# Reordered borders around the feed-forward stage of a transformer block kernel

## The reference

```
x1 = ln(x) * (1 + scale1) + shift1
x  = x + gate1 * (attention(x1 @ qkv_w + qkv_b) @ out_w + out_b)      # 16 heads of 128
x2 = ln(x) * (1 + scale2) + shift2
x  = x + gate2 * (gelu(x2 @ ffn_w1 + b1) @ ffn_w2 + b2)               # 256 -> 1024 -> 256
```

## Time and profile before

| | us |
|---|---|
| median of 3 runs (lowest, highest) | 1209.67 (1206.79, 1210.87) |
| the profiled execution's own time | 1212.73 |
| its span | 1211.0 |
| PE, DVE, ACT, POOL busy | 1148.2, 740.0, 649.9, 514.8 |
| first up product to last up product of ffn1 | 536.6 to 637.2 |

### The profile page before, as it was taken

How to read it: one execution, slowest core, us unless ns; L and a number is a source line. 1 busy time by engine, 2 the same in 40 slices (tenths; PEclk the granted TensorE clock), 3 DMA queues, 4 the chain that set the end, 5 groups by cost and what they waited for, 6 DMA issues and landing times.

```text
span 1211.0 us, 22481 instructions
## 1 busy us (share of the span) xinstructions
PE 1148.2 (95%) x7600; PEld 1017.2 (84%) x7632; DVE 740.0 (61%) x1633; ACT 649.9 (54%) x1839; POOL 514.8 (43%) x590
## 2 busy tenths in 40 slices
PE   6999999999999999989997999999999999987994
PEld 5888999999999999978886788888887888776894
DVE  3566654335443454357665786777777777776667
ACT  3455444444444444454553677665766666684452
POOL 4111131113111211142335676665676688663673
PEclk9999999999999999999998999999999999999997
DMA  9200000000000002022002007930000100032637
GB/s 333 75 1 1 19 1 19 1 1 1 1 18 1 1 1 87 1 105 105 19 18 71 1 1 203 292 99 1 10 23 6 49 18 19 14 83 90 180 114 232
DMA packets 47267, 70.08 MB, mean 58 GB/s; under 512 B 4279, under 2 KB 39355, under 8 KB 46171
## 3 DMA queue, kind: packets, MB, share of 16 engines
q1 hardware_dynamic: 43747, 60.21, 16.5%
q0 software_dynamic: 3408, 8.43, 1.9%
HBM read 40.24 MB, written 29.30 MB: 57 GB/s over the span
## 4 chain that ended last, share of the span: by engine, by line
PE 77%; DVE 4%; POOL 3%; issue 2%; ACT 2%; DMA 2%; SPq 0%; DVEq 0%; POOLq 0%; ACTq 0%
PE bank L1834 12%; PE bank L2023 10%; PE bank L1871 9%; PE bank L2080 7%; PE bank L1902 6%; PE bank L2170 5%; PE bank L1862 4%; PE bank L2106 4%; PE bank L1844 4%; PE bank L2213 3%; PE bank L2137 2%; PE bank L2145 2%; PE bank L2244 2%; PE bank L1852 2%; PE bank L1964 2%
## 5 line engine op out<-in xcount | busy, mean ns | idle before, releaser
L577 POOL TENSOR_TENSOR p<-p,rinv 128x512 f32<-128x512 f32 x64 | 66.6, 1040 | 410.1 <-DVE rinv L1384 410.1
L906 ACT ACTIVATE p<-bank,nb,rq 128x128 f32<-128x128 f32 x256 | 113.9, 455 | 89.4 <-DVE nb L1605 89.4
L778 ACT ACTIVATE p<-bank,nmax 128x128 f32<-128x128 f32 x256 | 90.7, 367 | 117.2 <-DVE nmax L1372 117.2
L650 POOL TENSOR_TENSOR qr<-qr,rb 128x512 f32<-128x512 f32 x64 | 81.7, 1276 | 82.0 <-DVE rb L1559 80.8
L1834 PE MATMUL bank<-cur_hi,wqk_hi 128*128 128x512 f32 x256 | 108.8, 425 | 4.5 <-DVE cur_lo L1325 4.5
L1380 DVE COPY pt<-bank 128x512 f32<-128x512 f32 x64 | 44.2, 691 | 107.2 <-PE bank L1852 104.4
L1834 PE MATMUL bank<-cur_hi,wqk_lo 128*128 128x512 f32 x256 | 101.9, 398 | 0.0
L1834 PE MATMUL bank<-cur_lo,wqk_hi 128*128 128x512 f32 x256 | 101.8, 398 | 0.0
L787 ACT ACTIVATE o_hi<-bank,bqkv 128x512 fp32r<-128x512 f32 x64 | 44.2, 691 | 101.2 <-PE bank L1862 100.9
L1388 DVE SCALAR_TENSOR_TENSOR o_lo<-bank,bqkv,o_hi 128x512 fp32r<-128x512 f32 x64 | 48.0, 751 | 53.7 <-ACT o_hi L787 53.7
L1862 PEld LDWEIGHTS bank<-pt,v 128*128 128x128 f32 x512 | 67.2, 193 | 13.0 <-DVE pt L1380 8.5
(11 more groups left out here) (279 smaller groups left out, 3733.7 us busy)
## 6 DMA issues: line engine op xcount, KB each, us to landing
token_scratch<-empty SPq DMA_DIRECT2D x1, 17415.0 KB, 65.2
xs<-token_scratch SPq DMA_DIRECT2D x39, 129.0 KB, 2.3
wqk_raw<-in_wqk SPq DMA_DIRECT2D x8, 512.0 KB, 10.4
gate<-gates_scratch SPq DMA_DIRECT2D x8, 512.0 KB, 3.8
got_t<-expert_scratch SPq DMA_DIRECT2D x16, 256.0 KB, 5.3
w_raw<-in_w SPq DMA_DIRECT2D x2, 1408.0 KB, 5.8
xres<-in_x SPq DMA_DIRECT2D x4, 512.0 KB, 9.7
wv_raw<-in_wv SPq DMA_DIRECT2D x8, 256.0 KB, 10.5
```

Source lines behind the costliest of these rows:

```text
L577: nc.gpsimd.tensor_tensor(p1[:, h % 2], p1[:, h % 2], rinv[:, h % 2].unsqueeze(2).broadcast_to([P, GB, T]), ALU.mult).then_inc(a_pn, 1)
L650: nc.gpsimd.tensor_tensor(qr[:, s.u % 2], qr[:, s.u % 2], rb[:], ALU.add).then_inc(g_qr, 1)
L778: last = nc.scalar.activation(p1[:, h % 2, b], bank[3][:, b * T:(b + 1) * T], ACT.Exp, bias=nmax[:, h % 2, b:b + 1], accum_out=rsum[:, h % ...
L906: last = nc.scalar.activation(p2[:, (s.u - 3) % 2, j], bank[3][:, j * T:(j + 1) * T], ACT.Exp, scale=rq[:, (s.u - 3) % 4, j:j + 1], bias=n ...
```

## The change

Five parts. (a) The splitting of three halves of the feed-forward weights moves into heads 11 to 15 of attention1's last group; ACT, DVE and POOL take them there. (b) The gated bias of attention1's last group moves into heads 8 to 11, one sequence in each head. (c) At the first border PE's order is changed: up product 0 stands ahead of values product 62, up products 1 and 2 among the last two heads' work; the low part `h_lo` moves to other memory and so waits for transposes instead of a values product. (d) In the feed-forward the gated bias of a group is one product and one addition of 1024 elements a partition instead of four pairs of 256; `residual_scale` waits for the product alone, `residual_add` for the addition. That of the last group moves into steps 1 and 2 of attention2, its scaling from step 2 to 3, its addition from step 5 to 6. (e) At the second border step 0 starts with keys, queries and values, down product 30 stands behind them and down product 31 behind the queries and transposes of step 1; DVE's wait for the bias goes. Tiny activations (`load_table`) make ACT load the table of Gelu and of Exp at places of their own. The diff, cut to its core:

```diff
-        gb2 = sb("gb2", [P, D], at=W + 114 * KB)
+        gb2 = sb("gb2", [P, GB, D], at=WORK + 12 * KB)
-        h_lo = sb("h_lo", [P, 2, GT], F32R, at=WORK + 8 * KB)
+        h_lo = sb("h_lo", [P, 2, GT], F32R, at=WORK + 16 * KB)
...
# POOL
+            def sequence_bias(g, b):
+                pool.wait_ge(d_gate, 16 * (g + 1))
+                if b > 0:
+                    pool.wait_ge(r_b, GB * g + b)
+                nc.gpsimd.tensor_tensor(gb1[:], gate[:, b], obias[:], ALU.mult).then_inc(r_gb, 1)
+                xs = xres[:, bass.ds(g * GB + b, 1), :].rearrange("p a d -> p (a d)")
+                pool.wait_ge(r_gb, GB * g + b + 1)
+                nc.gpsimd.tensor_tensor(xs, xs, gb1[:], ALU.add).then_inc(r_b, 1)
+            def gated_bias(g):
+                pool.wait_ge(d_small, 16 * 5)
+                pool.wait_ge(d_gate, 16 * (NG + g + 1))
+                if g > 0:
+                    pool.wait_ge(r_b, BIASED + g)
+                nc.gpsimd.tensor_tensor(gb2[:], gate[:], obias[:].unsqueeze(1).broadcast_to([P, GB, D]),
+                                        ALU.mult).then_inc(r_gb, 1)
+            def add_bias(g):
+                pool.wait_ge(r_gb, BIASED + g + 1)
+                xg = xres[:, g * GB:(g + 1) * GB]
+                nc.gpsimd.tensor_tensor(xg, xg, gb2[:], ALU.add).then_inc(r_b, 1)
...
+                    if g == NG - 1 and 8 <= h < 8 + GB:
+                        sequence_bias(g, h - 8)
+                    if g == NG - 1 and h == 12:
+                        pool.wait_ge(w_hi2, 1)
+                        nc.gpsimd.tensor_tensor(w1_lo[:, 0:NF // 2], w1_raw[:, 0:NF // 2],
+                                                w1_hi[:, 0:NF // 2].bitcast(F32), ALU.subtract).then_inc(w_lo2, 1)
-            pool.wait_ge(w_hi2, 1)
-            nc.gpsimd.tensor_tensor(w1_lo[:, 0:NF // 2], w1_raw[:, 0:NF // 2], w1_hi[:, 0:NF // 2].bitcast(F32),
-                                    ALU.subtract).then_inc(w_lo2, 1)
             normalise(NG * H - 1, 1)
-            residual_bias(NG - 1, NG - 1, gb1)
...
-            for g in range(NG):
-                pool.wait_ge(d_small, 16 * 5)
-                residual_bias(NG + g, g, gb2)
-                if g < NG - 1:
-                    norm(2 * NG + g, True)
+            for g in range(NG - 1):
+                gated_bias(g)
+                add_bias(g)
+                norm(2 * NG + g, True)
...
+                if s.first and s.u == 1:
+                    gated_bias(NG - 1)
+                if s.first and s.u == 2:
+                    add_bias(NG - 1)
...
# ACT
+                    if g == NG - 1 and h in (11, 12, 14):
+                        split2((h - 11) // 2, (h - 11) % 2 if h < 14 else 0)
...
+            def load_table(kind):
+                nc.scalar.activation(table[:], eps[:], kind)
...
-            split2(0, 0)
             act.wait_ge(n_ev, 2 * (NG + 1))
             act.wait_ge(a_vp, n)
             cur(NG, 0)
             exps(n - 1, 1)
-            split2(0, 1)
+            act.wait_ge(consts, 3)
+            load_table(ACT.Gelu)
             o_hi(n - 2, H - 2)
-            split2(1, 0)
...
                     if s.first:
                         h_round(NG * NF - 1, NF - 1, False)
+                        load_table(ACT.Exp)
...
-                    if s.first and s.u == 0:
-                        act.wait_ge(f_dp, NG * NF)
+                    if s.first and s.u == 4:
+                        act.wait_ge(r_b, BIASED + NG)
...
                 if i == 7:
+                    load_table(ACT.Exp)
                     logits_copy(NG - 1, bank[6])
...
# DVE
             def residual_scale(r, j):
-                dve.wait_ge(r_b, GB * (r + 1))
+                if r < NG:
+                    dve.wait_ge(r_b, GB * (r + 1))
+                else:
+                    dve.wait_ge(r_gb, BIASED + r - NG + 1)
...
             def residual_add(r, g):
+                if r >= NG:
+                    dve.wait_ge(r_b, BIASED + r - NG + 1)
...
+                    if g == NG - 1 and h in (13, 15):
+                        split2((h - 13) // 2, (15 - h) // 2)
...
             o_lo(n - 2, H - 2)
-            split2(0, 1)
             p_t(n - 1)
-            split2(1, 0)
-            o_lo(n - 1, H - 1)
...
-                elif f == 0:
-                    dve.wait_ge(a_pvp, n - 2)
+                else:
+                    dve.wait_ge(a_tp, n - 1 + f)
...
                 if s.first and s.u == 0:
-                    dve.wait_ge(r_b, GB * 2 * NG)
                     h_rest(NG * NF - 1, NF - 1, False)
-                if s.first and s.u == 2:
+                if s.first and s.u == 3:
                     dve.wait_ge(f_dp, NG * NF)
                     residual_scale(2 * NG - 1, 0)
                     residual_scale(2 * NG - 1, 1)
-                if s.first and s.u == 5:
+                if s.first and s.u == 6:
                     residual_add(2 * NG - 1, NG - 1)
...
# PE
             p_transposes(n - 2, H - 2)
-            values_product(n - 2, H - 2)
             pe.wait_ge(w_lo2, 1)
             pe.wait_ge(a_q, n)
             ffn_up(0, 0, True, NG)
-            out_product(n - 2, H - 2)
-            p_transposes(n - 1, H - 1)
-            values_product(n - 1, H - 1)
+            values_product(n - 2, H - 2)
             pe.wait_ge(a_k, n)
             ffn_up(1, 1, True)
+            p_transposes(n - 1, H - 1)
+            out_product(n - 2, H - 2)
+            values_product(n - 1, H - 1)
+            ffn_up(2, 2, True)
             out_product(n - 1, H - 1)
...
-                for f in range(2 if first else 0, NF):
+                for f in range(3 if first else 0, NF):
...
                     if s.u == 0:
-                        ffn_down(NG * NF - 2, NF - 2)
                         pe.wait_ge(w_lo3, 8)
...
                         if s.first and s.u == 0:
-                            ffn_down(NG * NF - 1, NF - 1)
+                            ffn_down(NG * NF - 2, NF - 2)
                         weighted_values()
...
+                if s.first and s.u == 1:
+                    ffn_down(NG * NF - 1, NF - 1)
```

More of the change, by code:

```diff
@@ L100, in program @@
         rinv = sb("rinv", [P, 2, GB])
+        table = sb("table", [P, 8])
         W = cursor[0]
@@ L378, in program @@
         W31_STEP = 13
+        BIASED = GB * NG
         def late_chunk(c):
@@ L452, in _ @@
             sp.dma_start(cos_sin[:], ins["cos_sin"]).then_inc(d_rope, 16)
-            sp.wait_ge(r_b, GB * NG)
+            sp.wait_ge(r_b, BIASED)
             sp.dma_start(obias[:], ins["b2"].partition_broadcast(P)).then_inc(d_small, 16)
@@ L561, in _ @@
                 nc.gpsimd.tensor_tensor(lo, raw, hi.bitcast(F32), ALU.subtract).then_inc(w_lo1p, 1)
-            def residual_bias(r, g, gb):
-                pool.wait_ge(d_gate, 16 * (r + 1))
-                for b in range(GB):
-                    nc.gpsimd.tensor_tensor(gb[:], gate[:, b], obias[:], ALU.mult).then_inc(r_gb, 1)
-                    xs = xres[:, bass.ds(g * GB + b, 1), :].rearrange("p a d -> p (a d)")
-                    pool.wait_ge(r_gb, GB * r + b + 1)
-                    nc.gpsimd.tensor_tensor(xs, xs, gb[:], ALU.add).then_inc(r_b, 1)
-                    if b < GB - 1:
-                        pool.wait_ge(r_b, GB * r + b + 1)
+            def sequence_bias(g, b):
[17 more added lines that the diff above has]
+                nc.gpsimd.tensor_tensor(xg, xg, gb2[:], ALU.add).then_inc(r_b, 1)
             def normalise(n, h):
@@ L585, in attention1 @@
                     if h == 0 and not first:
-                        residual_bias(g - 1, g - 1, gb1)
+                        for b in range(GB):
+                            sequence_bias(g - 1, b)
                     job = background_norm(g, h, first)
@@ L815, in attention1 @@
                         split_pair(h // 2 + 1)
-            attention1(0, True)
-            for g in range(1, NG):
-                attention1(g, False)
+                    if g == NG - 1 and h in (11, 12, 14):
+                        split2((h - 11) // 2, (h - 11) % 2 if h < 14 else 0)
             def split2(weights, half):
@@ L824, in split2 @@
                 act.wait_ge(d, 16)
+                act.wait_ge(a_kp, 3 * H + 10 + 4 * weights + 2 * half)
                 nc.scalar.activation(hi[:, fs], raw[:, fs], ACT.Copy).then_inc(w_hi2, 1)
+            attention1(0, True)
+            for g in range(1, NG):
+                attention1(g, False)
+            def load_table(kind):
+                nc.scalar.activation(table[:], eps[:], kind)
             def split3(c):
@@ L843, in _ @@
             n = NG * H
-            act.wait_ge(a_kp, n)
-            split2(0, 0)
             act.wait_ge(n_ev, 2 * (NG + 1))
@@ L863, in ffn1 @@
                     m = g * NF + f
-                    if f == 1 and first:
-                        o_hi(n - 1, H - 1)
                     if f >= 1 or not first:
@@ L874, in ffn1 @@
                     if f == 1 and first:
```

(2 more changed lines are left out.)

## The result

The changed kernel takes 1201.03 us (median of 6 runs, 1198.12 to 1202.91) against 1210.8 of the kernel before on the same chip: ratio 0.9923 [0.9908, 0.9938], 9.3 us faster by the ratio. One of the six runs of the kernel before took 2305.53 us; the ratio leaves it out. The forecast was 1195.0 in 1190.5 to 1203: faster, as said, and inside the range, but by 9 to 11 us and not 14.7. So the question is where some 3 to 5 us went.

A forecast was written before the change was run, and what follows sets the result against it. PE was taken as the bound, with time to gain only where it stands still or runs slowly. Terms 5.8 + 3.1 + 4.8 + 1.0 = 14.7 us took the median from 1209.67 to 1195.0 us, range 1190.5 to 1203.

The forecast's parts named there:

- First border: From attention 1's last heads to down product 0: waits and slow clock go, 5.8 us gained, bounds 3.0 to 6.1.
- What would show it: Signs of being right; at the first border, down product 0 11.5 us behind head 62's transposes, at clock 1.0.
- The heads' covers: Bias and weight pieces moved into attention 1's heads are hidden there: cost 0, or 14.0 us without cover.
- heads longer than 7.83: Sign of being wrong: heads 11 to 15 of attention 1 taking longer than 7.83 us.
- Inside the feed-forward: PE's 3.4 us of `gate` waits go, less 0.3 for held `h_lo`: 3.1 us gained, bounds 0 to 3.4.
- Second border: Feed-forward into attention 2: head start 6.9, less 0.6 and a slow stretch of 1.5: 4.8 us gained, bounds 1.0 to 6.3.
- Behind it: Attention 2 after the second border: moving the residual addition one step gains 1.0 us, bounds -1.0 to 2.3.
- The border that gives nothing: Rival: at the second border POOL's pieces, scaling and slow clock use up the head start; 1200.8 us, chance 0.14.
- the gain taken back whole: Rival: a later transfer or engine takes the gain back, at most 3.6 us left; 1206 to 1210, chance 0.05.
- the slower case: Rival: eight large POOL pieces of 2.36 us hold DVE on the path; 4.2 us slower, 1213.9, chance 0.03.
- full clock throughout: Rival: no slow stretches, so the terms sum to 17.8 us and the time is 1191.9 us; chance 0.12.
- The drain of the tables: Rival: a table load standing alone costs a drain too, 1.3 us more at the first border; 1196.3, chance 0.03.

The follow-up runs named there:

- before_again: The kernel before, word for word, profiled once more on a second chip: 1207.93 us.
- e1: The kernel before with only an unused 32-byte tile a partition added ahead of the weights: 1213.02 us, ratio 1.0014 to the kernel before.
- second pair: Profiles of the unedited kernel before and the unedited changed kernel, taken again on a second chip: 1207.93 and 1198.79 us.
- e6: The changed kernel with the last group's gate scale and residual add moved behind the maxima of their own steps: 1195.67 us, ratio 0.988 to the kernel before.
- after_again: The changed kernel, word for word, run and profiled again on a second chip: 1198.79 us, ratio 0.9906 to the kernel before.
- e7: The changed kernel with GpSimd's addition of the gated bias cut into four pieces: 1199.33 us, ratio 0.9915 to the kernel before.
- e13: The changed kernel with the table tile behind all others, scale and addition behind the maxima, last gated product at step 0's end: 1196.83 us, ratio 0.9885.

## Why the prediction came out as it did

**First border, 5.8.** Right: 5.6 by undoing it, 5.5 and 4.6 by pairs. What would show it (11.5 behind the transposes, no `pt` wait, full clock) stood at 11.8, 0 and 1.00. The 4.6 comes from before_again, whose border was 16.35: some 1.0 of the 5.8 is a slow stretch that the kernel before doesn't have in every execution.

**The heads' covers, 0.** Right for the moved pieces. But a cost of 2.0 us in attention 1 stood in no term: I priced `load_table` by its instructions and never its tile, and "from there to the end every stage is shifted as a whole" had no counterpart for what lies before. This is the term missing from the sum. A sign of being wrong did come with it, heads longer than 7.83: they took 7.87, but so did the heads of the groups before, and not only 11 to 15.

**Inside the feed-forward, 3.1.** 3.9 and 3.3. The `gate` waits went whole, and the 0.3 for held `h_lo` tiles was not paid. The larger of the two is above my bound of 3.4.

**Second border, 4.8.** 6.1 and 4.7. I counted one slow stretch of 1.5 in it; in the recorded profile none stands before the keys of step 4, and the one I meant falls just behind them (651.6 to 655). The step-through at full clock gave 6.3, and the first pair shows 6.1. But the changed kernel's stretch is the steady one (24.24, 24.23); that of the kernel before was 30.31, 28.92 and, with the pad of e1, 28.62, the longest with two slow stretches in it. So 4.8 fits the second pair by some luck: my 18.4 and the head start were read from the longest. The first exponentials came 6.1 earlier against up product 31 in the one pair and 4.7 in the other, forecast some 6.

**Behind it, +1.0.** The step that failed. -1.0 and -2.7. "It moves one step; I take 0.7 of the wait": the keys' wait did fall (2.9 to 0.7, 2.6 to 1.5 in the second pair), but the scores of step 3 come hardly sooner by it (12.50 behind the keys of step 4, 12.61 in before_again), and I never asked what stands behind the addition in its new place. There the scores of step 4 come 8.3 behind those of step 3, in before_again 7.1. My own lower bound named it ("the addition is paid in the next step"); where the clock falls behind the new wait it is 1.6 more. Likewise I had the scaling in step 3 only waiting for its product, not standing ahead of `nmax`. e6 shows what this order costs, in both steps: 1.8 us by itself, 3.4 with the slow stretch that followed it in after_again, 3.1 by the medians. The 1.0 of it that is the scaling's belongs to the second border's term.

**From profile to median.** Even the stretches' 14.5 of the recorded pair did not reach the medians. The profiled execution of before was 3.1 above its median, and I kept these 3.1 for after. But next to before_again (1207.93) it is 3.0 us longer from the transposes of head 62 to the scores of step 7 alone (174.83 against 171.86), in slow stretches that the change was to remove. I took the excess out with them and put it in the baseline too. By the second pair the changed stretches give 9.9; with attention 1's -2.0 and the experts' load (1.4 of a wait) that is 9.3, and the ratios give 9.3 and 11.4. That they meet so well is in part luck: behind the scores of step 7 the two profiles of the changed kernel took 505.6 and 502.0 us, those of the kernel before 504.9 and 504.3. From 1060 to 1120 us the changed kernel's clock was 0.86 in the one and 0.94 in the other.

**The rivals.** The border that gives nothing, the gain taken back whole, and the slower case did not come; nor did full clock throughout, though e7's profile shows that it can come in this stretch. What the slower case rests on is real, though: large POOL pieces do hold DVE (2.60, 2.48, 2.48), three times under cover in the feed-forward, and on the path in e13, where one cost 2.2. GPSIMD Engine Reference of the Trainium skill (Key points) names the same contention for instructions of two SBUF inputs, and the trace agrees: the scaling, which reads PSUM, took 1.27 for its two instructions in e6, though POOL's addition of 2.37 began 0.09 behind its start, and 1.28 in the feed-forward, where POOL was free. The drain of the tables did not come either: the first activation began 0.01 behind the load's end (533.49 + 1.28, 534.78), and the exponentials' work ahead of the load ended 0.02 before it, so the 2.66 us of ScalarE: Activation LUTs (What ACT_TABLE_LOAD costs) is again not borne out.

## What to carry to other kernels

When work is moved out of one engine's chain, look at what stands behind it in the new place; here putting it behind the instruction that others wait for (the maxima) was worth 3.1 us, and moving it a step nothing that could be shown. Put a large GpSimd instruction where no VectorE instruction of the critical chain that reads two SBUF tiles can begin under it; an idle GpSimd is not enough. Where a new tile can stand behind the old ones, put it there, and compare a stretch that no edit touches: it is the cheapest control there is. And a slow stretch in one profile of the kernel before is not a gain to count on; look for it in a second profile first.

## What was not expected of the hardware

Moving the weights and work tiles by 32, 64 or 128 bytes made 56 heads of PE-bound work 1.9 to 2.3 us longer (449.35 against 451.28 to 451.64), with no wait added; profiles of one placement agree to 0.1 us across three chips. The cause was not found. Stretches at 1.2 GHz do not follow a long wait of PE each time. In the 14 profiles PE stood 29 times for 2.0 to 3.3 us between 500 and 700 us, and the clock fell 16 times: behind the wait of step 3 (some 2.35) in 2 of the 9 profiles that have it, behind that of step 6 (2.06 to 2.30) in 5 of 8. Even behind the stall of 3.07 at the first border, which before_again has as the recorded profile has, it stayed at 1.00 there. So one profile of a kernel can be 1 to 3 us shorter than the next in such places alone.
